# A decoder layer on one core: GpSimd adds the fourth key tile of the softmax sums too

## What is computed

```python
x = x + self_attention(layernorm(x))      # 16 heads of 32, 512 keys, q k v o with biases
x = x + cross_attention(layernorm(x), ctx)  # 16 heads of 32, the first 512 rows of ctx, causal mask
x = x + mlp(layernorm(x))                 # 512 -> 2048 -> 512, gelu
# attention, per head:
p = exp((q @ k.T) * scale - max)          # 512 queries x 512 keys
out = (p @ v) / p.sum(over keys)
```

## Time and profile before

| | us |
|---|---|
| median of 3 runs | 1180.89 |
| lowest and highest | 1178.44, 1182.04 |
| the profiled execution, its own time | 1178.57 |
| its span, first to last instruction | 1176.8 |
| PE busy in it | 1138.1 (97%) |
| DVE busy | 670.4 (57%) |
| ACT busy | 485.4 (41%) |
| POOL busy | 432.8 (37%) |

### The profile page before, as it was taken

One profiled execution on the slowest core, in us unless ns is written; L12 is line 12 of the kernel. 1 busy time (PEld: TensorE's weight loads), 2 busy tenths in 40 slices (PEclk: granted clock), 3 DMA queues, 4 the chain that ended last, 5 costly groups with the idle time before them and its releaser, 6 DMA issues.

```text
span 1176.8 us, 15866 instructions
## 1 busy us (share of the span) xinstructions
PE 1138.1 (97%) x6016; PEld 770.9 (66%) x6016; DVE 670.4 (57%) x966; ACT 485.4 (41%) x792; POOL 432.8 (37%) x398
## 2 busy tenths in 40 slices
PE   5999999999999999999999999999999999999998
PEld 4745666656656554666666666557887887887886
DVE  5776767677676667667668667654534224134212
ACT  4365454456545655645635545552321111111110
POOL 1256534443556765344454556663101001001000
PEclk9999999999999999999999999999999999999999
DMA  6933433333334444435345445411310000000000
GB/s 233 285 103 91 115 124 83 95 108 90 91 103 143 118 126 127 138 107 163 109 124 141 137 126 171 116 46 38 97 54 36 1 1 36 0 0 29 7 1 36
DMA packets 73735, 110.30 MB, mean 94 GB/s; under 512 B 6976, under 2 KB 45888, under 8 KB 71744
## 3 DMA queue, kind: packets, MB, share of 16 engines
q1 hardware_dynamic: 70864, 102.00, 29.2%
q0 software_dynamic: 2080, 6.82, 2.1%
q10 hardware_dynamic: 720, 0.54, 0.1%
HBM read 71.58 MB, written 37.75 MB: 93 GB/s over the span
## 4 chain that ended last, share of the span: by engine, by line
PE 88%; ACT 4%; DVE 2%; issue 2%; POOL 2%; DMA 1%; SPq 0%; DVEq 0%; ACTq 0%; POOLq 0%
PE PS L951 18%; PE PS L952 17%; PE PS L953 17%; PE PS L1084 11%; PE PS L1069 10%; PE PS L1047 9%; ACT PT L870 1%; PE PS L965 1%; PE PS L1050 1%; PE PS L1072 1%; ACT stackQ L855 1%; PE PS L1079 1%; POOL P_sum L734 1%; DVE m_cols L1290 1%; DMA stackK<-scratch 1%
## 5 line engine op out<-in xcount | busy, mean ns | idle before, releaser
L1290 DVE TENSOR_REDUCE m_cols<-PS 128x1 f32<-128x512 f32 (+3 forms) x432 | 282.3, 668 | 150.4 <-PE PS L1047 75.7
L870 ACT ACTIVATE PT<-PS 128x512 f32<-128x512 f32 (+1 forms) x432 | 238.8, 581 | 189.7 <-PE PS L1069 76.5
L734 POOL TENSOR_TENSOR P_sum<-PT 128x512 f32<-128x512 f32 x128 | 161.7, 1283 | 306.1 <-ACT PT L870 306.1
L1069 PE MATMUL PS<-stackQ,stackK 100*128 100x512 f32 (+3 forms) x512 | 182.1, 403 | 12.3 <-ACT PT L870 12.0
L1047 PE MATMUL PS<-stackK,stackQ 96*128 96x512 f32 (+3 forms) x512 | 179.0, 386 | 2.5 <-DVE m_cols L1290 1.3
L923 ACT ACTIVATE hid<-PS,b1c 128x512 f32<-128x512 f32 x64 | 44.1, 690 | 279.7 <-PE PS L953 277.7
L1371 DVE CAST hidH<-hid 128x512 fp32r<-128x512 f32 x64 | 28.8, 451 | 224.6 <-ACT hid L923 221.9
L1069 PEld LDWEIGHTS PS<-stackQ,stackK 100*128 100x128 f32 x512 | 90.7, 190 | 88.3 <-ACT PT L870 40.1
L1298 DVE RECIPROCAL P_sum<-PS 128x512 f32<-128x512 f32 x32 | 107.4, 3358 | 42.9 <-PE PS L1084 42.9
L1047 PEld LDWEIGHTS PS<-stackK,stackQ 96*128 96x128 f32 x512 | 91.9, 190 | 51.7 <-DVE m_cols L1290 23.1
L740 POOL TENSOR_TENSOR P_sum<-P_sum,PT 128x512 f32<-128x512 f32 x96 | 120.8, 1284 | 8.8 <-ACT PT L870 4.6
(11 more groups left out here) (124 smaller groups left out, 1782.0 us busy)
## 6 DMA issues: line engine op xcount, KB each, us to landing
scratch<-stage SPq DMA_DIRECT2D x128, 256.0 KB, 2.5
stackK<-scratch SPq DMA_DIRECT2D x62, 256.0 KB, 4.0
stackQ<-scratch SPq DMA_DIRECT2D x46, 256.0 KB, 3.9
stackQ<-scratch SPq DMA_DIRECT2D x18, 512.0 KB, 4.8
stackK<-scratch SPq DMA_DIRECT2D x60, 128.0 KB, 4.4
stackQ<-scratch SPq DMA_DIRECT2D x28, 128.0 KB, 3.7
PT<-wT SPq DMA_DIRECT2D x3, 1024.0 KB, 8.7
x_res<-x SPq DMA_DIRECT2D x3, 1024.0 KB, 9.3
```

The costliest lines, as they stand in the source:

```text
L734: pool.tensor_tensor(P_sum[:, h, :], PT[:, h, :], PT[:, 4 + h, :], ALU.add).then_inc(p_added, 1)
L870: nc.scalar.activation(PT[:, slot:slot + heads, q0:SEQ], PS[:, T_BANK + n % 2, 0:heads * width].rearrange("p (h n) -> p h n", h=heads), AC ...
L1069: mm = nc.tensor.matmul(dst[:, a, :], stackK[0:STACK + HPG, par, h + a, k * P:(k + 1) * P], stackQ[0:STACK + HPG, par, h + a, q0:SEQ], sta ...
L1290: nc.vector.tensor_reduce(m_cols[:, q, STACK + h:STACK + h + heads], PS[:, S_BANK + m % 2, 0:heads * n].rearrange("p (h n) -> p h n", h=he ...
```

## The change

POOL adds the probabilities of k = 3 to `P_sum` too: four adds of 128 x 512 in a self unit, one of 4 x 128 queries for all heads in a cross unit. They stand behind the adds of k = 2 and ahead of the rest of POOL's work in the unit. `sum_rows` keeps its first set of four matmuls and loses the second. It waits, as before, for all of the unit's adds, which are now more.

```diff
 def adds_before(u):
     cross = max(u - FIRST_CROSS, 0)
-    return (u - cross) * 2 * HPG + cross * (HPG + HPG // ADD_HEADS[CROSS])
+    return (u - cross) * 3 * HPG + cross * (HPG + HPG // ADD_HEADS[CROSS] + 1)

 def adds_until(u, k, h):
-    return adds_before(u) + (h + 1 if k == 1 else HPG + h // ADD_HEADS[layer_of(u)] + 1)
+    return adds_before(u) + (h + 1 if k == 1 else (k - 1) * HPG + h // ADD_HEADS[layer_of(u)] + 1)
...
             def add_probabilities(u, k, h):
-                heads = ADD_HEADS[layer_of(u)] if k == 2 else 1
+                heads = 1 if k == 1 or layer_of(u) == SELF else ADD_HEADS[CROSS] if k == 2 else HPG
                 pool.wait_ge(p_ready, fills_until(u, k, h + heads - 1))
...
                     if h == 0:
-                        pool.wait_ge(p_added, adds_until(u, 1, HPG - 1))
+                        pool.wait_ge(p_added, adds_until(u, 1, HPG - 1) if k == 2 else
+                                     adds_before(u + 1) - (HPG if layer_of(u) == SELF else 1))
                     q0 = queries(u, k)
                     sums = P_sum[:, h:h + heads, q0:SEQ]
-                    pool.tensor_tensor(sums, sums, PT[:, h:h + heads, q0:SEQ], ALU.add).then_inc(p_added, 1)
+                    slot = (4 * k + h) % 8
+                    pool.tensor_tensor(sums, sums, PT[:, slot:slot + heads, q0:SEQ], ALU.add).then_inc(p_added, 1)
...
                 for h in range(0, HPG, ADD_HEADS[layer_of(u)]):
                     add_probabilities(u, 2, h)
+                for h in range(HPG if layer_of(u) == SELF else 1):
+                    add_probabilities(u, 3, h)
                 for n in raws_of(u, 9.0, 99.0):
                     low_raw(n)
...
             def sum_rows(u):
-                q0 = queries(u, KT - 1)
                 pe.wait_ge(p_added, adds_before(u + 1))
-                four_heads(R_BANK, 0, lambda h: ones[:, :], lambda h: P_sum[:, h, :], True, False)
-                four_heads(R_BANK, q0, lambda h: ones[:, :], lambda h: PT[:, 4 + h, q0:SEQ],
-                           False, True).then_inc(p_used, 1)
+                four_heads(R_BANK, 0, lambda h: ones[:, :], lambda h: P_sum[:, h, :], True, True).then_inc(p_used, 1)
```

## The result

| | before | after |
|---|---|---|
| median | 1179.68 | 1184.68 |
| lowest and highest of 10 | 1178.44, 1182.90 | 1183.53, 1188.46 |
| PE busy in the profiled execution | 1138.1 | 1131.9 |
| POOL busy | 432.8 | 533.2 |

A forecast was written before the change was run, and what follows sets the result against it. PE was busy for 97% of the span, but ACT's copies of the maxima limit gains at turns. -6.4 + 4.0 + 3.3 = +0.9 on 1178.57, plus 2.3 to the median of runs, gave 1181.8; range 1174.5 to 1187.

The forecast's parts named there:

- products 0.43 apart behind the stalls: Sign of being wrong: PE's products behind units 0 and 12 at the prologue's lower-clock pace.
- granted clock at 1.0 throughout: Sign of being right: PE's clock stays at its upper level for the whole execution.
- turns: Ends of units: of 17.6 us removed from PE, 6.4 passes, limited by ACT's copies of the maxima before the first exponential.
- unit 0, wait for root(1): POOL's root(1) ends 5.1 later behind four adds, delaying ACT's first normed and the turn: +4.0, once.
- unit 12, load 5: Load 5 is issued four adds later, high_raw(5) on ACT waits, the next first exponential comes late: +3.3, once.
- PE waits for POOL's adds: Row sums: tightest self units leave 0.9 of room after four more adds, so the wait is priced at 0.
- The two stalls: Waits in unit 0 for root(1), +4.0, and in unit 12 for load 5, +3.3.
- I don't take it: Clock fall while PE stands in units 0 and 12, 2.4 each, left out of the sum as the waits are short.
- no other such gap: Claim that the trace shows no other clock fall because PE has no gap like the prologue's.
- the loads of later units have their buffer filled long before: Claim that only unit 12's load is delayed by the adds, so that stall happens once.
- the clock falls in the stalls: Rival: PE's clock falls in both stalls, units 0 and 12, 2.4 each: +5.7, 1186.6; chance 0.15.
- the likeliest case: The forecast itself, everything as priced within 0.3%: 1178.5 to 1185; chance 0.50.

The follow-up runs named there:

- the set alone: Kernel before without the second set of row sums and without new adds, so the fourth key tile is missing from the sums: 1173.30, ratio 0.9942.
- the cross units alone: The change made in cross units only, self units as in the kernel before: 1180.28, ratio 1.0004.
- the fastest kernel: Changed kernel with unit 12 as before, root(1) first, unit 28's low halves under place 12 ahead of its add, values of k = 3 behind the turn: 1168.33, ratio 0.9907.
- the chosen units: New adds and single set of row sums only in self units except unit 12, root(1) ahead of the adds, elsewhere as before: 1173.20, ratio 0.9943.
- the late values: Self units except 12 changed, root(1) first, plus values of k = 3 moved between transposition of the maxima and row sums in all units: 1169.82, ratio 0.9920.
- with both sets: Changed kernel with the second set of row sums kept on PE beside the new adds: 1191.35, ratio 1.0095.
- with root(1) first: Changed kernel with root(1) of unit 0 ahead of the four new adds: 1179.08, ratio 0.9993.
- with the raws first: Changed kernel with the low halves of weights with place under 12 ahead of the new adds in units 12 and 28: 1182.08, ratio 1.0020.
- with both: Changed kernel with root(1) of unit 0, and the low halves of weights under place 12 in units 12 and 28, ahead of the new adds: 1176.62, ratio 0.9980.

## Why the prediction held in its range, and where its account failed

The forecast was 1181.8 and 1184.68 was measured. The change itself was put at +0.9 and came to +5.0. The two distances differ because the forecast stood on a median of three runs (1180.89) that lay 1.2 above the later median of ten; that part of its nearness is luck. Of its own signs of being wrong one came, products 0.43 apart behind the stalls; of its signs of being right "granted clock at 1.0 throughout" failed.

| step | predicted | measured |
|---|---|---|
| turns | -6.4 | -6.2 (the set alone) |
| unit 0, wait for root(1) | +4.0 | +4.0 |
| unit 12, load 5 | +3.3 | +3.5 (loads 5 and 6) |
| PE waits for POOL's adds | 0 | 0 (a weight load 0.3, hidden) |
| clock in both stalls | 0 | +1.4 and +1.1 (by the traces) |
| unit 28, a load | 0 | +1.1 |
| unit 30, clock | 0 | +3.1 in the profiled execution |

**The turns** were right, and in their parts too. From the start of the row sums to the next exponential, units 3, 7, 11 and 15 gave 0.86 to 0.87 each, the units like 6 gave 0.13 to 0.14, cross units nothing, but for unit 30 with 0.07. That the gain ends at ACT's copies is shown three ways: by the set taken out alone, by the cross units alone, and by the turn of the fastest kernel, where other work fills the wait.

**The two stalls** were right in place and size, and unit 0 in its cause. At unit 12 load 5 is only the first cause: moved ahead, it left most of the stall to load 6, which the prediction has on ACT's path but doesn't price as late. POOL was in time at the row sums. In unit 14, the tightest, its adds of k = 2 and 3 ended at 453.16, 0.66 ahead of the first matmul of the row sums at 453.82:

```profile
444.23 8.93 POOL L743 TENSOR_TENSOR P_sum<-P_sum,PT 128x512 f32<-128x512 f32 x7
```

**The step that failed** is the sentence on the clock, "I don't take it". I had reasoned that 17 us of little work stood ahead of the low pace in the prologue, and 3 us of waiting here. Both stalls brought the clock down. The price that I had for it, 2.4 each, was too large: it was 1.4 and 1.1. A likely reason, not tested by itself, is that PE partly waits for ACT at the lower clock anyway (0.54 and 0.32 behind the stall of unit 13). The two falls, 2.5, are the larger part of the 4.1 that the sum missed. The prediction also gave "no other such gap" as the reason why the trace before shows no other fall; the falls in units 14, 15 and 30 of other traces came without such a gap, so that isn't the whole condition. The second part is "the loads of later units have their buffer filled long before": in unit 28 `high_raw` waited 1.91 for such a load before, and the cross add, 1.3 long, stands ahead of its issue now. The row that says so:

```profile
745.72 0.63 ACT L849 ACTIVATE FH<-raw 128x512 fp32r<-128x512 f32 x1 [1.91 <-DMA raw<-p2T]
```

It is a row of the kernel before; I had looked at two places in POOL's queue and not at all of them. In the changed kernel the issue and the use are each 6.0 later, where the row sums of unit 27 are 4.9 later:

```profile
748.77 0.57 POOL L713 DMA_DIRECT2D raw<-p2T  x1 [0.31 <-POOL FL L718]
...
751.76 0.63 ACT L854 ACTIVATE FH<-raw 128x512 fp32r<-128x512 f32 x1 [3.00 <-PE PS L958]
```

The bracket names PE, but the load was issued 2.99 ahead of this row, and before it was 2.98, so it is most likely the load that ended the wait.

With 2.5 and 1.1 the sum would have been 0.9 + 3.6 = 4.5 above the kernel before; 5.0 was measured. The rival "the clock falls in the stalls" (chance 0.15) is the case that happened, with the price of each fall about half; that the time also lies in the interval of the likeliest case, 1178.5 to 1185, doesn't make that case right.

**What stays open.** Why the clock falls in unit 14, 15 or 30 in some executions, with PE at work most of the time and without a wait of a microsecond. It happened in unit 14 of the kernel without the second set too (25.33 instead of 22.85), so the new adds aren't needed for it. Waits of 0.89 at the turns are in all the traces where I saw it, but also in those of kernels where it didn't happen, the chosen units for one, and I tried nothing on that. The kernel before isn't free of it either, by its runs: of 72 on the chips of the experiments, the 10 with a mean granted clock of 1.000 have a median of 1178.4, the 14 with 0.997 or less 1181.2; the two with 0.995 must have had a longer stretch at the lower clock than the traced one, and no trace shows where. Whether the three longer runs of the changed kernel all had the fall of unit 30 isn't shown. And the expectation for the late values, 9.6, was met by a third; the cost in the first units of batches explains part of it, and taking it out there brought the cost up elsewhere.

## What to carry to other kernels

Before counting removed work as gain, look at what another engine does in the same time and what both meet in: here PE's second set stood in the shadow of ACT's copy, and a third of it counted. Work that is given to an idle engine goes behind everything in its queue that others wait for; go through every later item of that queue (signals, and issues of loads), not only the nearest. A wait of 2.3 to 3.2 us on PE cost more than itself here, since the clock fell behind each of them; and a place where PE waits for a fixed chain is a place to put work into, once it is clear what that work covered where it stood.

## What the hardware did that I hadn't expected

- The clock fell behind every wait of PE between 2.27 and 3.18 in the traces of all runs, eight in five kernels (3.02 and 3.18; 2.98 and 2.27 with both sets; 3.10 with root(1) first; 2.98 and 2.53 with the raws first; 2.60 with both). By the windows of the changed kernel it was granted 0.72 to 0.75 on average over 12 to 13 us. It didn't fall behind the waits of 1.12 to 1.45 in unit 28. It also fell where no wait ahead was above 0.9, in stretches that cost 2.1 (unit 15 of two kernels), 2.5 (unit 14 without the second set) and 3.1 (unit 30).
- The same load of 256 KB from POOL's queue isn't there after the same time: load 5 took 4.6 from issue to use before and 3.05 in the changed kernel, and the load of unit 28 2.9 to 4.4. Where the buffer's reader waits for it, that spread is as large as the effects looked for.
- Eight adds back to back on POOL took 10.17 in unit 0, 10.18 in unit 14 and 10.14 in unit 15, 1.27 apart, with DVE and ACT at work beside them; the shortest and the longest of the changed kernel's 176 adds took 1.27 and 1.30.
